# GNN, two layers on one core: the last group's gathers cover 40 partitions, and POOL's last round is written out

## Time and profile before

| what | us |
|---|---|
| median of 3 timed runs | 4208.57 (4202.96 to 4210.07) |
| profiled execution, its own time | 4207.65 |
| its span | 4205.7 |
| POOL busy | 3064.9 (73%) |
| PE busy | 3147.9 (75%) |
| DVE busy | 2322.7 (55%) |
| ACT busy | 798.6 (19%) |

### The profile page before, as it was taken

One profiled execution on the slowest core, in us unless ns is written; L12 is line 12 of the kernel. 1 busy time (PEld: TensorE's weight loads), 2 busy tenths in 40 slices (PEclk: granted clock), 3 DMA queues, 4 the chain that ended last, 5 costly groups with the idle time before them and its releaser, 6 DMA issues.

```text
span 4205.7 us, 55810 instructions
## 1 busy us (share of the span) xinstructions
PE 3147.9 (75%) x13605; PEld 2400.0 (57%) x13705; DVE 2322.7 (55%) x5665; ACT 798.6 (19%) x1490; POOL 3064.9 (73%) x3229
## 2 busy tenths in 40 slices
PE   7888788898888888889876666666666666666666
PEld 5666666676666666767554444444444444444544
DVE  5444444344444443434476666666666666766676
ACT  2222222222222222222240000010110111111112
POOL 7777777777777777767347777777777777777775
PEclk9999999999999999999897777877878778788777
DMA  5555555455545454545245555555555555555554
GB/s 186 154 157 155 155 158 157 151 158 153 154 149 166 152 153 148 168 140 163 74 128 157 160 157 156 161 160 160 162 156 165 161 161 164 160 165 161 160 169 122
DMA packets 321499, 651.40 MB, mean 155 GB/s; under 512 B 149711, under 2 KB 170425, under 8 KB 321465
## 3 DMA queue, kind: packets, MB, share of 16 engines
q0 software_dynamic: 150528, 414.45, 34.3%
q1 hardware_dynamic: 164448, 230.16, 17.5%
q10 hardware_dynamic: 6489, 6.40, 0.5%
HBM read 637.67 MB, written 13.08 MB: 155 GB/s over the span
## 4 chain that ended last, share of the span: by engine, by line
POOL 30%; PE 23%; issue 18%; DMA 12%; DVEq 7%; DVE 6%; ACT 2%; ACTq 1%; POOLq 1%; SPq 0%
POOL rows L377 30%; PE psum L865 7%; PE psum L854 7%; DMA rows<-z_tab,idx 6%; DMA rows<-in_x,idx 5%; DVEq L731 4%; DVE rows L972 2%; PE psum L851 1%; PE psum L584 1%; PE psum L874 1%; DVEq L727 1%; PE psum L909 1%; PE psum L896 1%; PE psum L1217 1%; PE psum L901 1%
## 5 line engine op out<-in xcount | busy, mean ns | idle before, releaser
L377 POOL DMA_INDIRECT rows<-in_x,idx x1568 | 1510.2, 963 | 531.8 <-issue 450.0
L377 POOL DMA_INDIRECT rows<-z_tab,idx x1568 | 1503.6, 959 | 482.5 <-issue 455.5
L972 DVE TENSOR_TENSOR rows<-rows,psum 128x1024 f32<-128x1024 f32 x392 | 478.5, 1221 | 1153.7 <-DMA rows<-in_x,idx 803.3
L584 PE MATMUL psum<-rows,onehot 128*128 128x260 f32 x3136 | 1059.5, 511 | 23.6 <-issue 23.3
L584 PEld LDWEIGHTS psum<-rows,onehot 128*128 128x128 f32 x3136 | 805.8, 263 | 208.8 <-issue 32.0
L854 PE MATMUL psum<-weights,edge_room 128*128 128x256 f32 x3136 | 816.7, 384 | 6.3 <-issue 1.5
L865 PE MATMUL psum<-rows,onehot 128*128 128x256 f32 x3136 | 776.9, 393 | 0.0
L854 PEld LDWEIGHTS psum<-weights,edge_room 128*128 128x128 f32 x3136 | 607.3, 194 | 161.1 <-issue 8.2
L952 ACT ACTIVATE rows<-rows 128x1024 f32<-128x1024 f32 x392 | 414.3, 1057 | 1491.7 <-DVE rows L972 1491.6
L865 PEld LDWEIGHTS psum<-rows,onehot 128*128 128x128 f32 x3136 | 602.3, 197 | 78.1
L801 DVE TENSOR_TENSOR rows<-rows,psum 128x1024 f32<-128x1024 f32 x392 | 460.7, 1216 | 77.9 <-ACT psum L673 77.9
(11 more groups left out here) (152 smaller groups left out, 1787.6 us busy)
## 6 DMA issues: line engine op xcount, KB each, us to landing
dst_t<-in_dst_jp SPq DMA_DIRECT2D x197, 512.0 KB
edge_room<-in_edge_t SPq DMA_DIRECT2D x196, 512.0 KB, 3.9
rows<-in_x,idx POOLq DMA_INDIRECT x1568
rows<-z_tab,idx POOLq DMA_INDIRECT x1568
dst_t<-in_x_t SPq DMA_DIRECT2D x28, 448.0 KB, 5.3
z_tab<-edge_room SPq DMA_DIRECT2D x14, 455.0 KB, 3.5
idx<-in_src_idx SPq DMA_DIRECT2D x392, 4.0 KB, 1.6
out<-onehot ACTq DMA_DIRECT2D x13, 448.0 KB, 3.4
```

What stands on the lines that cost most here:

```text
L377: nc.gpsimd.indirect_dma_start(rows[:, u, j, 0:width], None, table, bass.IndirectOffsetOnAxis(ap=idx[:, u, j:j + 1], axis=0)).then_inc(L.r ...
L584: last = pe.matmul(agg_ps[0:WIN, 0:width], onehot[:, hot, j, :], rows[:, u, j, 0:width], start=(j == 0), stop=(j == J - 1))
L972: dve.tensor_tensor(half, half, psum[:, 2 * b:2 * b + 2, :].rearrange("p b (j d) -> p (b j) d", j=2), ALU.add).then_inc(added, 1)
```

## The change

`gather` takes a count of partitions, and the new function `filled(g)` gives it: 40 where g is the constant 195, 128 otherwise. For g to be a constant, POOL's last round must not be in the loop, so `rounds` takes `peeled`, and POOL's calls pass 1: the loop runs one round less, and the last round's four groups (32 gathers with their waits) are written out behind it. In group 195 the partitions 40 to 127 of `rows` keep what group 191 left there; their edges are padding. No other engine's program changes.

```diff
-        def rounds(eng, body, finish_nodes=None, ends=0, begun=False):
+        def rounds(eng, body, finish_nodes=None, ends=0, begun=False, peeled=0):
...
             if finish_nodes is None:
-                return until(0, ROUNDS - 1)
+                until(0, ROUNDS - 1 - peeled)
+                for n in range(ROUNDS - peeled, ROUNDS):
+                    for u in range(RING):
+                        body(n, u, n * RING + u)
+                return
...
+        def filled(g):
+            return -(-(EDGES - (GROUPS - 1) * GROUP) // J) if isinstance(g, int) and g == GROUPS - 1 else P
...
-        def gather(L, table, width, u):
+        def gather(L, table, width, u, count=P):
             for j in range(J):
                 nc.gpsimd.indirect_dma_start(
-                    rows[:, u, j, 0:width], None, table,
-                    bass.IndirectOffsetOnAxis(ap=idx[:, u, j:j + 1], axis=0)).then_inc(L.rows_in[u], 16)
+                    rows[0:count, u, j, 0:width], None, table,
+                    bass.IndirectOffsetOnAxis(ap=idx[0:count, u, j:j + 1], axis=0)).then_inc(L.rows_in[u], 16)
...
-                gather(L, table, width, u)
-            rounds(pool, body, begun=begun)
+                gather(L, table, width, u, filled(g))
+            rounds(pool, body, begun=begun, peeled=1)
...
-                gather(layer0, t["x"], D, u)
-            rounds(pool, body, begun=True)
+                gather(layer0, t["x"], D, u, filled(g))
+            rounds(pool, body, begun=True, peeled=1)
```

## The result

The changed kernel takes 4184.21 us (median of 5, 4180.57 to 4189.08), the kernel before 4208.57 us (median of 5, 4200.05 to 4210.07). The ratio is 0.9948, 95% interval 0.9934 to 0.9963. The forecast of 4208.2 us and its range from 4202 to 4214 missed it. The profiled execution has a span of 4183.4 us, 22.3 us less than before.

A forecast was written before the change was run, and what follows sets the result against it. The prediction took POOL's gathers to bound layer 1 and PE the end of layer 0. From the 4208.57 us median it took 0.41 us for layer 1's last group and 0 for the rest: 4208.2 us, range 4202 to 4214.

The forecast's parts named there:

- Only 16 of these 3136 gathers change: Gathers of both layers: only 8 at each layer's end change, so only what waits for those 16 was costed.
- Last group of layer 1: End of layer 1: eight gathers of 40 partitions land sooner and remove DVE's wait, a gain of 0.41 us.
- t: POOL's time for one 40-partition gather, taken as 0.63 us; the 0.41 us gain holds below 0.90 us.
- the landing: Layer 1's last group: rows arrive 4.93 us after the last gather's start, the same for short gathers.
- The queues' load is not on any wait: DMA descriptors: 16 gathers carry 88 rows less each, which was to change the time by 0 us.
- Last group of layer 0: End of layer 0: DVE adds group 195 earlier, but PE is the bound there, gain 0.
- the written-out round: POOL's last round in both layers: loop count and branch go, but POOL's queue hides them, 0 us.
- Rival A: Normalisation between the layers: moved code removes POOL's 2.81 us stop before L1150, giving 4205.4 us; chance 0.14.
- Rival B: Normalisation loop: the moved stop returns at each of six turns, 14.1 us more at most, 4222.3 us; chance 0.05.
- Rival B's other sign: Layer 0's loop: a group's second gather repeatedly comes late, 1.87 us idle for 0.30, so stops can return with loops.
- Rival C: Short gathers: 40 partitions cost as much as 128 or more, giving 4208.6 to 4213.7 us; chance 0.08.
- Rival D: PE's last sum at the end: it falls in a slow clock stretch, adding 2.3 us, 4210.5 us; chance 0.11.

The follow-up runs named there:

- i1: The changed kernel with one unused gather of 128 partitions added behind its last group; 4206.81 us against 4207.86 for the kernel before, ratio 1.0001.
- e1: The change without its 40-partition gathers: POOL's last round written out in all four places, every gather 128 partitions; ratio 1.0007 to the kernel before.
- f3: The same kernel as e1, run again; ratio 1.0000 to the kernel before.
- i2: The kernel before with one unused gather of 48 partitions added behind its last group; 4191.73 us against 4207.86, ratio 0.9960.
- g2: The kernel before with eight unused gathers of 40 partitions added behind its last group; 4186.17 us against 4207.49, ratio 0.9950.
- h2: The kernel before with one unused gather of 8 partitions added behind its last group; one run, 5461.09 us against 5464.36.
- f1: The changed kernel run again as it is, on a chip where gathers are not the bound; ratio 0.9996 to the kernel before.

## Why the prediction was wrong

**The step that failed** is the first sentence on which all others stand: "Only 16 of these 3136 gathers change", and with it a sum that has no term for the other 3120. They changed. Groups of the changed kernel (busy us and mean ns of one, then idle time ahead of them by what ended it), and below them those of the kernel before:

```profile
L384 POOL DMA_INDIRECT rows<-z_tab,idx x1568 | 1496.8, 955 | 482.8 <-issue 452.7 <-DVEq L738 25.0 <-DMA idx<-in_src_idx 5.1
L384 POOL DMA_INDIRECT rows<-in_x,idx x1568 | 1488.4, 949 | 536.8 <-issue 447.2 <-PE psum L861 88.6 <-DMA idx<-in_src_idx 1.0
```
```profile
L377 POOL DMA_INDIRECT rows<-in_x,idx x1568 | 1510.2, 963 | 531.8 <-issue 450.0 <-PE psum L854 80.9 <-DMA idx<-in_src_idx 1.0
L377 POOL DMA_INDIRECT rows<-z_tab,idx x1568 | 1503.6, 959 | 482.5 <-issue 455.5 <-DVEq L731 21.9 <-DMA idx<-in_src_idx 5.1
```

Layer 0: 1510.2 - 1488.4 = 21.8 us less busy, of which 536.8 - 531.8 = 5.0 us come back as idle time: 16.8 us, where 16.7 were measured at the gathers' starts. What grew are the waits for PE to free the group's buffer (80.9 to 88.6): the faster gathers meet a consumer that was just behind them. Layer 1: 6.4 us less busy up to the last group and 0.3 us more idle (482.5 to 482.8): 6.1 us, as measured. Its waits for VectorE's queue (21.9 and 25.0) took nothing back. None of them is longer than 0.3 us, which is what lies between any two gathers, and what they have more "issue" has less. The short gathers' own part in the busy time is 0.3 us in layer 0 and 0.5 us in layer 1. A single trace of the kernel before does not show that a gather's time has a second value; but the trace did say that the gathers are the pace of most of the span (POOL 30% of the chain, layer 1, once begun, without a wait over 0.3 us), and that 1 ns on each of them is 3.1 us. A range that took that in would have been wider on both sides.

**Last group of layer 1.** Right in result, the 0.41 us of DVE's wait, but two terms were mis-sized and their errors ran against each other. i1 shows what the change is worth without mode B: nothing that 11 runs can tell from 0 (1.0001, interval 0.9992 to 1.0010). The first term is t: the gathers of 40 partitions took 0.90 to 0.96 us here, 0.92 on average, not 0.63. The last one started at 4151.29, 8.56 us behind the group's first, where the eight full ones took 4175.01 - 4166.03 = 8.98 us. POOL saved 0.42 us, not the 2.5 that the forecast has. The second term is the landing, which was kept at 4.93 us. With that the rows would have been there at 4151.29 + 4.93 = 4156.22 us and DVE, which read them at 4156.09, would still have waited for 0.13 us (the forecast's own limit for t was 0.90 us). They were there sooner: the gathers' queue shows its last packets over by 2.2 us behind the last start and none from 4153.5 to 4156.1. In the kernel before the queue was still busy 4.6 us behind it, with some 150 packets (of 48 a gather) from 4175.0 to 4179.9. So the 4.93 us were in good part a backlog of full gathers, and the sentence "The queues' load is not on any wait" is wrong: it was on this one. DVE had hardly moved (its reduction starts 13.04 us behind the group's first gather, 13.21 before).

**Last group of layer 0** and **the written-out round**: 0 and 0, as forecast, within what i1 resolves for all parts together. e1 and f3 have ratios of 1.0007 and 1.0000, but ran where the gathers are not the bound. The crossing into the written-out code shows nothing: in layer 1 no gather of the last 32, the first at 4112.55, waited over 0.31 us.

**Rival A and B** rested on the 2.81 us stop between the layers, which the moved code would take away or repeat. It is where it was, and once:

```profile
2087.58 0.22 POOL L1157 TENSOR_TENSOR edge_room<-edge_room 112x16 f32 x1 [2.80 <-issue]
```

About 90 instructions more ahead of it (the forecast's estimate) did not move it. Nor does a transfer of instructions fall into it: from 2102.2 to 2105.1 us of the kernel before and from 2084.7 to 2087.7 us of the changed one the DMA shows packets of the queue q1 alone, and none of the queues of kind "instruction". So the rule of the Trainium skill that was cited for it (Runtime: NRT & Kernel Launch, Instruction fetch mechanics) does not explain this stop; what POOL stood still for is open. Rival B's other sign, the 1.87 us ahead of a group's second gather in layer 0's loop, is not the loop's either. It stands in the written-out round too:

```profile
2005.90 0.94 POOL L384 DMA_INDIRECT rows<-in_x,idx  x1 [5.90 <-PE psum L861]
2008.72 0.94 POOL L384 DMA_INDIRECT rows<-in_x,idx  x1 [1.88 <-issue]
```

**Rival C** (40 cost as much as 128) was nearly right on the size: 0.93 us in layer 0's last group and 0.92 in layer 1's, of 0.957. **Rival D** happened in the changed kernel's profile (5.43 us at a granted clock of 0.69) and not in i1 (3.75 us at 1.00). It does not need the change: i2, which has nothing of it, shows 5.43 us too, and all other 18 profiles 3.74 or 3.75.

On the spread over engines, the packets of the kernel before and of the changed one, all of them and those of the gathers' queue:

```profile
DMA packets 321499, 651.40 MB, mean 155 GB/s; under 512 B 149711, under 2 KB 170425, under 8 KB 321465
q0 software_dynamic: 150528, 414.45, 34.3%
DMA packets 321245, 649.96 MB, mean 155 GB/s; under 512 B 149807, under 2 KB 170521, under 8 KB 321209
q0 software_dynamic: 150272, 413.00, 34.7%
```

The queue has 256 packets less, 16 for each short gather (48 to 32). But those under 512 B are 96 more, 6 for each short gather, so the queue's large ones are 22 fewer for each (16 + 6): a full gather has 32 of four rows and 16 small ones, a short gather 10 of four rows and 22 small ones. Ten packets of four rows are what the rule of the Trainium skill (DMA: Bandwidth & Descriptors, Why a DMA increments its semaphore by 16 and not by 1) gives for 40 partitions, ten engines with four rows each. The trace agrees with it, though no row names the engines. That the landing would not be later was right as well.

## What to carry to other kernels

Before a change to a few instructions of a kind that sets the pace is costed, compute what one nanosecond on all of them is worth, and when the result is off, compare the medians of the untouched ones first. A landing time that is read behind a row of full transfers holds their backlog; it is not a constant to carry over to short ones. Cut both spans at the same events, so that the sum of the parts is the difference. To learn whether an edit works by what it does or by something beside it, put the suspected side effect alone on the old kernel (g2) and take it out of the new one (i1).

## What the runs showed that was not expected

- One gather of 8, 40, 48 or 120 partitions at the very end of a launch goes with full gathers that take 946 to 949 ns (layer 0, 1024 bytes a row) and 953 to 957 ns (layer 1, 1040 bytes a row) in place of 957 to 960. With 64 or 128 at the end they stay. What is left behind, and why layer 1 gains less, is open.
- POOL's time for a gather hardly depends on its partitions: 957 ns for 128 (median), 914 for 64 and 912 to 927 for 40 (means of eight in a last group), against 0.957 x 40/128 = 0.30 us in proportion. Single ones took 896 ns for 8 (h2), 886 for 48 (i2) and 987 for 120 (h3). Shortening a gather saves next to nothing of POOL's time; no run tried fewer gathers.
- On three of five chips the same kernel took 1.3 times as long, with waits of up to 21.3 us (ScalarE in f1) that no instruction of the program explains, so no gain of 0.5% could be seen there. What the waits are is open.
